# A graph network kernel: the node stage in a loop of two groups, and the fourth message of the edge network behind the first sum of gathered rows

## The reference

```python
edge_index = jnp.stack([src, dst])
# layer 0: attention over the edges (4 heads of 64), per node a softmax over incoming edges and the node itself
x = _layernorm(x + gat(x, edge_index, edge_attr_32, ...))
# layer 1: an edge network, and the mean of its output per src node
h = jnp.concatenate([x[src], x[dst]], axis=-1)
h = jnp.tanh(h @ W0 + b0)
h = jnp.tanh(h @ W1 + b1)
h = h @ W2 + b2
h = h * (edge_attr_128 @ Wg)
x = _layernorm(x + segment_mean(h, src))
```

## Time and profile before

| | |
|---|---|
| time before, median of 3 runs | 5690.76 us (5681.23 to 5723.21) |
| the profiled execution's own time | 5656.99 us |
| its span, first to last instruction | 5655.2 us |
| mean granted TensorE clock in it | 0.909 of full speed |
| node stage | from 2229 to 3395 us of the span |
| edge network | from 3395 to 5346 us |
| busy share of the span, PE / DVE / ACT / POOL | 76% / 67% / 57% / 58% |

### The profile page before, as it was taken

The page is one execution under the profiler, slowest core; times in us unless marked ns, Lnnn a source line. Parts: engine busy times, 40 slices in busy tenths (PEclk is TensorE's granted clock), DMA queues, the critical chain, the costliest instruction groups (busy, mean ns, idle before and its releaser), DMA issues. The chain is left out here.

```text
span 5655.2 us, 82150 instructions
## 1 busy us (share of the span) xinstructions
PE 4294.2 (76%) x24476; PEld 3452.5 (61%) x24476; DVE 3801.3 (67%) x12195; ACT 3244.0 (57%) x7255; POOL 3284.4 (58%) x3036
## 2 busy tenths in 40 slices
PE   6777777777567674898898987998888989989600
PEld 3455555555344442888888885777777777777500
DVE  7766666666566665888887865666666666666564
ACT  7655555555344332555555555666666666666575
POOL 0255555656566664444444436777777777777532
PEclk9999999999888876999999998999999999999855
DMA  3222222222275554999999985666666666666597
GB/s 81 59 78 85 86 80 83 86 85 82 66 180 166 163 163 149 311 334 329 327 332 325 333 299 131 146 139 141 136 139 140 140 139 144 142 140 143 123 398 279
DMA packets 774416, 976.13 MB, mean 173 GB/s; under 512 B 182069, under 2 KB 685148, under 8 KB 761084
## 3 DMA queue, kind: packets, MB, share of 16 engines
q0 software_dynamic: 170176, 323.19, 25.6%
q10 hardware_dynamic: 269085, 374.19, 18.8%
q1 hardware_dynamic: 334715, 273.49, 15.9%
HBM read 541.99 MB, written 429.16 MB: 172 GB/s over the span
## 5 line engine op out<-in xcount | busy, mean ns | idle before, releaser
L1371 PE MATMUL bank<-w0r,n_x1T 128*128 128x406 f32 x4704 | 916.8, 353 | 84.2 <-ACT n_pa L1419 58.9
L1371 PEld LDWEIGHTS bank<-w0r,n_x1T 128*128 128x128 f32 x4704 | 869.9, 190 | 118.6 <-issue 76.6
L1570 PE MATMUL bank<-u_h,w1r 128*108 128x512 f32 (+1 forms) x2646 | 733.7, 425 | 0.0
L1518 POOL DMA_INDIRECT out_x<-u_sums,u_row x392 | 632.9, 1615 | 147.0 <-issue 117.1
L570 POOL DMA_INDIRECT DS<-by_dst,rank_int x392 | 376.2, 960 | 569.9 <-DVE rank_int L740 429.0
L396 PE MATMUL bank<-wst,xT 128*128 128x264 f32 x2352 | 406.8, 311 | 254.5 <-DVE xps L405 193.2
L396 PEld LDWEIGHTS bank<-wst,xT 128*128 128x128 f32 x2352 | 329.9, 199 | 441.1 <-issue 321.7
L1500 POOL DMA_INDIRECT u_pa<-PA,u_rows x392 | 409.5, 1045 | 264.6 <-PE bank L1558 121.5
L1570 PEld LDWEIGHTS bank<-u_h,w1r 128*108 128x108 f32 (+1 forms) x2646 | 469.8, 184 | 142.7
L822 POOL DMA_INDIRECT xg<-XP,m_src x392 | 426.8, 1089 | 215.7 <-issue 107.2
L1247 POOL DMA_INDIRECT n_cg<-CT,n_last x392 | 423.4, 1080 | 174.7 <-issue 96.3
(11 more groups left out here) (286 smaller groups left out, 10649.4 us busy)
## 6 DMA issues: line engine op xcount, KB each, us to landing
PA<-n_pa ACTq DMA_DIRECT2D x98, 816.0 KB, 4.5
PB<-n_pb ACTq DMA_DIRECT2D x98, 812.0 KB
XP<-xps ACTq DMA_DIRECT2D x98, 528.0 KB
CT<-ct ACTq DMA_DIRECT2D x98, 528.0 KB
n_xp<-XP SPq DMA_DIRECT2D x98, 528.0 KB
xin<-in_x SPq DMA_DIRECT2D x97, 512.0 KB
n_x<-in_x SPq DMA_DIRECT2D x97, 512.0 KB
out_x<-n_x ACTq DMA_DIRECT2D x97, 512.0 KB, 3.8
```

The source lines that it names most:

```text
L1371: o = nc.tensor.matmul(acc, xT[s][p][:, k, e], w0r[q][:, 2 * half + k, :], start=(n == 0), stop=(n == len(terms) - 1))
L1518: pool.indirect_dma_start(out=out, out_offset=bass.IndirectOffsetOnAxis(ap=si[s][:, j:j + 1], axis=0), in_=yo[s][:, j, :], in_offset=None, ...
L1570: o = nc.tensor.matmul(acc, a[p], b[q], start=(start and n == 0), stop=(stop and n == 2))
```

## The change

Two edits. First, a second way of writing a list, `looped`, is added, and the node stage uses it on all five engines. It writes out groups 0 to 3, then a loop that runs 46 times over a pair of groups (groups 4 to 95), then groups 96 and 97. Each engine has its own loop and its own counter; no barrier stands between iterations. In the loop `g` is a register's value, so semaphore values and addresses that depend on it are computed by the engine's sequencer. No instruction of the bodies and no order within them is changed. Second, in DVE's body of the edge network `add_first` of group g+2 stands ahead of the fourth message instead of behind it.

```diff
+    def looped(eng, body):
+
+        for g in range(2 * PEEL):
+            body(g, g % 2, g // 2, False)
+        with eng.Fori(PEEL, PAIRS - 1) as i:
+            for s in range(2):
+                body(i * 2 + s, s, i, False)
+        for s in range(2):
+            body(2 * PAIRS - 2 + s, s, PAIRS - 1, s == 1)
...
-                    groups(sp, body)
+                    looped(sp, body)
...
-                    groups(pool, body)
+                    looped(pool, body)
...
-                    groups(dve, body)
+                    looped(dve, body)
...
-                    groups(pe, body)
+                    looped(pe, body)
...
-                    groups(act, body)
+                    looped(act, body)
...
                         low_message(g, s, 0)
                         message(g, s, 2)
                         low_message(g, s, 1)
-                        message(g, s, 3)
                         if not late(g, 2):
                             add_first(g + 2, s, i + 1)
+                        message(g, s, 3)
                         low_message(g, s, 2)
                         low_message(g, s, 3)
```

## The result

The changed kernel takes 5500.55 us (median of 3 runs, 5493.40 to 5534.84) against 5690.76. The profiled execution's span is 5498.8 us against 5655.2. The profiled execution of the kernel before was quicker than each of its three timed runs, so the two traces differ by 156 us where the medians differ by 190; the traces can't say where the other 34 us are. All lines of the new kernel stand 10 higher, so L1277 is now L1287.

The account below looks back on a forecast made before the run. The prediction took DMA first, then DVE and PE, to bound the node stage, and PE's stall the edge network. Order -82, computed values +5 and code -1 made -78, scaled to -79: 5612 us from 5690.8; 8-in-10 range 5575 to 5720.

Parts of the forecast that it names:

- The order's term: Edge network: the sum ahead of the fourth message shortens PE's stall, 19.45 to 18.6 us a group, -82 us.
- PE's next wait: Edge network: PE next limited by DVE's second low part of layer 0 (L1759), with 0.30 us of slack.
- POOL's floor of 18.48 us: Edge network: POOL's own work per group, untouched by DVE's order, limiting the gain to -93 us.
- The bound is DMA first: Node stage: a pair's transfers (22.75 us) fill the DMA engines; DVE and PE come second at 20.1 us a pair.
- The part on the loop: Node stage: computed values cost +5 us, the branch nothing, and less fetched code gives -1 us.
- bounds 0 and 1.6: Node stage: limits, in us a group, on the delay from DVE's computed values; 0.1 was taken.
- The branch, hidden at nothing: Node stage: DVE's loop branch runs behind the body's last 1.22 us instruction, costing 0, bounds 0 and +152 us.
- the 0.1 us of DVE's computed values: Node stage: sequencer computation delays DVE 0.1 us a group, half of it lost, +5 us in all.
- Rivals B and C: Node stage: DVE's branch must fetch code, half swallowed (5680 us, chance 0.22) or nothing swallowed (5764 us, chance 0.12).
- Less code fetched, -1 us: Node stage: the loop fetches 0.38 MB less code of one queue, about 1 us at 330 GB/s.
- Rival D: Edge network: the reorder does little, as the fourth message waits behind the sum's gather; 5680 us, chance 0.12.
- the node stage's bounds: Node stage: the loop's branch costs between 0 and +152 us over 46 iterations.

Follow-up runs that it names:

- e8: Against the kernel before: node stage on all five engines as 23 loops of two iterations each, edge network in the old order; ratio 0.9826.
- e7: Kernel before, without loops, plus nine satisfied waits ahead of each of SP's two loads and ACT's two table stores per node-stage group; ratio 0.9998.

## Why the prediction was wrong

**The order's term, right in mechanism and near in size on this chip.** -82 us forecast, -69.5 measured. The stall fell from 1.8 to 0.62 us (0.5 said), the clock rose to 0.99, and stretches of lower clock fell from 38 to 6 (counted in the trace's record of the clock). The average came to 18.73 and not 18.6, since 16 of 90 groups still take over 19.7 us, where hardly any was said. PE's next wait is at L1759, as named. POOL's floor of 18.48 us was read from one pair of gathers and is near: the distance between its first gathers of two groups is now 18.59 us in the median, and 18.37 or less in one of ten. That it was a floor of this one chip, about 18.0 on the second kind, no row of one trace could tell.

**The failed step: "The bound is DMA first".** It rested on the DMA share of 0.99 at 330 GB/s. The share counts how long packets were under way, not how many the engines could have moved: with the same packets it went to 1.04 at 361 GB/s. From this false bound followed that nothing on the issuing side could be worth anything. The Trainium skill (Perfetto Trace Analysis, Identifying the Most-Contended Engine) says to judge DMA by HBM utilization instead of occupancy, since 16 DMA engines make occupancy misleading; the two readings of 330 and 361 GB/s agree, and it was a rule that should have been weighed here.

**What the step left out.** The part on the loop costed DVE, PE, SP and POOL and didn't mention ACT's three stores. And it took for granted that a delay costs nothing or something: "bounds 0 and 1.6". A later start of a transfer also frees the engines for another one, and here that one was on the path. The rows for it were at hand: the earlier trace rows show a short and a long group, the prediction says that they alternate, and it put the long ones down to full engines without asking why every second gather should be early. With the issue times of the short group (0.26 us between the gather and PA's store) the sign at least would have been open. The size could hardly have been told: 0.39 us gives 75 us, and 0.72 us beyond the changed kernel's gives 27 back.

**The branch, hidden at nothing, and the 0.1 us of DVE's computed values: right.** Rivals B and C (5680 and 5764 us) are refuted, by the timeline at the branch, and by e8, where 23 loops begin. The Trainium skill (Runtime: NRT & Kernel Launch, Instruction fetch mechanics) says that a taken branch to code outside the blocks kept waits for a fetch; the loop over a pair of groups shows no such wait, with one block of each kind fetched in 940 us, and e8, whose 23 loops lie one behind the other, shows no such stall either.

**Less code fetched, -1 us: too small.** The term counted the bytes of one queue at the mean rate, and left out the larger one beside it:

```profile
q8 instruction: 40, 0.66, 0.3%
```

More than the bytes it is their place that counts: a 16,384-byte block holds one DMA engine for 1.1 us, and the group behind a gather that meets one is 0.8 to 1.8 us longer. The traces put that at 20 to 40 us of the stage.

**Rival D** (the sum's wait for the gather holds the fourth message) didn't happen on the chip of the prediction and did on the second kind. **The range** missed since no case in it had a gain from the loop of more than 1 us: the node stage's bounds were 0 to +152 us on top of the order's.

## What to carry to other kernels

A DMA share near 1 wasn't a bound here; look at GB/s in short and in long periods, and where periods alternate, look for the two transfers whose starts lie within a few tenths of a microsecond. A bulk store that started 0.3 us into the issue of a gather held up that gather here. With a start 0.4 us later the last row landed 1.0 us earlier, and the engine that waits for it went on 1.7 us earlier. Find the best distance by trying, since a store that starts too late loses the gain as well. Look also for code that is fetched while such a gather is under way. A loop or any edit that shifts issues by tenths of a microsecond moved a stage by 8% here, so a change's by-effects on timing are tested best by delays alone, behind the wait that releases the transfer.

## What was not expected of the hardware

- The same kernel took 5146, 5551 or 5698 us in different sets of runs, two of them under one chip number. The node stage, written out, is 1176 to 1194 us in all of them, while the stage ahead of it that ends at 1497 us here took 1298 us on the first kind and 1025 on the second.
- One 16,384-byte block of code that moves while a gather is under way goes with a wait for that gather that is 1.8 us longer (4.0 against 2.2 us, medians of 81 and 159 groups), though the block held one of 16 engines for 1.1 us.
- Of two transfers on different queues, the store that started 0.69 us ahead of the end of the gather's issue moved 439 rows of 1632 bytes in the next 3 us, and the gather 34 packets of 4224 bytes.
- A DMA with its address in a register starts 0.14 us later behind its wait than one with a constant (0.17 against 0.03 us behind ACT's last instruction). With all of ACT's list so written, the output store starts at 7.02 against 6.78 us, and PA's at 9.37 against 8.94.
- Two stores issued right behind one another: the second's issue took 0.53 us, and 0.37 us with 0.3 us between them (e7).
